# Feature products of a graph-attention layer in 32-column tiles, four side by side, in place of 64-column tiles

## The chip, the core and the metric

The kernel runs on one core of a Trainium2 chip. The metric is the device time of one execution in microseconds (us). Before the change it is 2252.53 us, the median of three runs (2251.53 to 2253.24).

## What is computed

Four graph layers follow each other on N = 2708 nodes with 256 features; each adds its result to its input and normalizes the sum over the features. The change lies in the last of them, a graph attention with 4 heads of 64 channels:

```
x = _layernorm(x + _L3_gnn_ref(x, adj, W, a_src, a_dst, bias))

def _L3_gnn_ref(x, adj, W, a_src, a_dst, bias):
    h = (x @ W).reshape(n, 4, 64)
    s_src = jnp.einsum('nhc,hc->nh', h, a_src)
    s_dst = jnp.einsum('nhc,hc->nh', h, a_dst)
    e = jax.nn.leaky_relu(s_src[:, None, :] + s_dst[None, :, :], 0.2)
    e = jnp.where((adj > 0.5)[:, :, None], e, -1e9)
    alpha = jax.nn.softmax(e, axis=0)
    return jnp.einsum('ijh,ihc->jhc', alpha, h).reshape(n, 256) + bias
```

All is float32, apart from masks. The first three layers are a gated layer with three attention heads, a normalized adjacency product and a second attention layer; they fill the first 1870 us or so and stay as they are.

## The kernel before, in words

Each engine runs a list of instructions written out by hand, and semaphores tie the lists together. In the last layer the exponentials are factored: an edge's weight is the larger of two products of a factor of the source node and one of the target node, times a mask. A factor of the source is moved out of the weight, into the projected features and into the denominators' operand.

The work is divided into three **sweeps** over the target nodes (`CW` = 3, column chunks `c` of 1024, 1024 and 660 targets) and, in each sweep, 22 **units**, one for each tile `t` of 128 source nodes (the last tile has 20). A unit is `n = c * 22 + t`, 66 in all. In each unit:

- SP loads the unit's strip of the adjacency into one of three buffers. ACT turns it into a mask (`above` L1466, `masked` L1473). In sweep 1 ACT also scales the tile's projected features (L1459), and before that it lays the source factors out as `g3`, 32 equal columns for each head.
- VectorE makes the weights of the four heads, `PM3` (L2085), each 128 sources by the sweep's targets, in one of three buffers: unit n waits until TensorE has finished unit n - 3 (`l3_mm`, L2078), and for the mask. Each head raises `l3_p`.
- TensorE multiplies. The **features**, L1150: for heads 0 and 1, then 2 and 3, and for each half of the targets (512 and 512 columns, in sweep 3 512 and 148), the stationary operand is 64 columns of `proj3`, one head, and the moving one that head's weights. The two heads of a pair write partitions 0 to 63 and 64 to 127 of one bank. The **denominators**, L1161: for each half, four products with 32 columns of `g3`, one for each head, which write partitions 0 to 31, 32 to 63 and so on of a bank. The last one raises `l3_mm`.

The trace has two weight loads and two products for each float32 product of the program, so a unit has 16 records of loads and 16 of products on L1150, and as many on L1161. Products of tiles that lie side by side in the array run at the same time.

The sums stay in six banks over a sweep: features of heads 0 and 1 in banks 0 and 1, of heads 2 and 3 in 2 and 3, denominators in 4 and 5. At a sweep's first unit each pair of banks is opened by a product of full width with zeros (`opened`, L880), after ACT has copied out the banks of the sweep before (`chunk_out`, L1481, after the last unit's `l3_mm`). After units 3, 7, 11 and 15 of sweeps 2 and 3 TensorE transposes two tiles of the sweep before back (`backs`, L1134), of which VectorE makes divisors (`divisors`, L2040 to L2046), ACT scaled rows (L1490), POOL a term for nodes without edges (L821, L823), and VectorE sums, statistics and the normalized rows (`added` L2053 on, `normed` L2068 on). VectorE does these between its weights, after units 5, 7 and 9 of each group of four. The tiles of the last sweep are finished behind the last unit.

Of the kernel before, what the change touches and what calls it, by code (L numbers as in the profile page):

```python
# [18 lines left out]
P = 128  # L19
# [5 lines left out]
T = -(-N // R)  # L25
# [12 lines left out]
C2, C3 = D // H2, D // H3  # L38
DQ = P // H3
# [10 lines left out]
BANK = 512  # L50
# [33 lines left out]
def kp(t):  # L84
    return R if t < T - 1 else TAIL
# [50 lines left out]
def wide(c):  # L136
    return min(WW, N - c * WW)
# [34 lines left out]
def build(nc, x, adj, gat_W, gat_a, e_Wih, e_Whh, e_bih, e_bhh, n_Wih, n_Whh, n_bih, n_bhh,  # L172
          W1, b1, W2, a2, W3, a_src, a_dst, b3, out):
    V, S, G, PE = nc.vector, nc.scalar, nc.gpsimd, nc.tensor
# [13 lines left out]
    with ExitStack() as ctx:  # L188
# [5 lines left out]
        def sb(*shape, dt=F32):  # L194

            n = int(np.prod(shape))
            words = n if dt == F32 else (n + 1) // 2 if dt == BF16 else (n + 3) // 4
            a = arena[:, top[0]:top[0] + words]
            top[0] += words + words % 2
            assert top[0] <= ARENA, top[0]  # L200
            if dt != F32:
                a = a.bitcast(dt)[:, 0:n]
            if len(shape) > 1:
                names = "abcd"[:len(shape)]
                a = a.rearrange(f"p ({' '.join(names)}) -> p {' '.join(names)}", **dict(zip(names, shape)))
            return a
# [143 lines left out]
        proj3 = sb(T, D + 2 * H3)  # L350
# [5 lines left out]
        PM3 = sb(3, H3, WW)  # L356
# [6 lines left out]
        def bank(i, n=1):  # L363
            return psum[:, i:i + n, :].rearrange("p b n -> p (b n)")
# [92 lines left out]
        def pair_at(n, first):  # L457

            c, t = divmod(n, T)
            if c and t >= first and (t - first) % 4 == 0 and (t - first) // 4 < DT // 2:  # L460
                return (c - 1) * DT // 2 + (t - first) // 4
            return None
# [415 lines left out]
        def opened(b):  # L878

            PE.matmul(bank(b), zrow[:, 0:P], zrow, start=True, stop=True)  # L880

        @block.tensor
        def _(pe):
# [137 lines left out]
            for n in range(UNITS):  # L1021
                c, t = divmod(n, T)
# [32 lines left out]
            for t in range(T):  # L1055
# [4 lines left out]
                for g in range(2):  # L1060
# [4 lines left out]
                    for kk in range(KD):  # L1065
# [5 lines left out]
                                        skip_group_check=True)  # L1071
# [25 lines left out]
            for n in range(UNITS):  # L1097
                c, t = divmod(n, T)
# [9 lines left out]
            for n in range(UNITS):  # L1108
                c, t = divmod(n, T)
# [5 lines left out]
                for h in range(H2):  # L1115
                    pe.wait_ge(l2_p, n * H2 + h + 1)
                    for r, nr in enumerate(blocks2(c)):
# [3 lines left out]
                                        start=k // 3 not in begun, stop=t == T - 1, skip_group_check=True)  # L1121
# [7 lines left out]
            def backs(v):  # L1129
                if v:  # L1130
                    pe.wait_ge(fin_scaled, v)
                for i, g in enumerate((2 * v, 2 * v + 1)):
                    for k in range(RAW3):
                        ins = PE.transpose(bank(6 + i)[0:kp(g), k * P:(k + 1) * P], rawT3[:, k, g % DT * R:g % DT * R + kp(g)], ident)  # L1134
                ins.then_inc(back_ps, 1)
            for n in range(UNITS3):
                c, t = divmod(n, T)
                halves = [(v, min(BANK, wide(c) - v * BANK)) for v in range(-(-wide(c) // BANK))]
                for h in range(0, H3, 2):
                    if t == 0:  # L1140
                        if c:
                            pe.wait_ge(l3_read, RAW3 * (c - 1) + h // 2 + 1)
                        for v, w in halves:
                            opened(h + v)
                    if c == 0:
                        pe.wait_ge(l3_scaled, t + 1)
                    pe.wait_ge(l3_p, n * H3 + h + 2)
                    for v, w in halves:
                        for g in range(2):
                            PE.matmul(bank(h + v)[g * C3:(g + 1) * C3, 0:w], proj3[0:kp(t), t, (h + g) * C3:(h + g + 1) * C3],  # L1150
                                      PM3[0:kp(t), n % 3, h + g, v * BANK:v * BANK + w], start=False, stop=t == T - 1, skip_group_check=True)
                if t == 0:
                    if c:
                        pe.wait_ge(l3_read, RAW3 * c)
                    else:
                        pe.wait_ge(l3_g, 1)
                    for v, w in halves:
                        opened(4 + v)
                for v, w in halves:
                    for h in range(H3):  # L1160
                        ins = PE.matmul(bank(4 + v)[h * DQ:(h + 1) * DQ, 0:w], g3[0:kp(t), t, h, :],  # L1161
                                        PM3[0:kp(t), n % 3, h, v * BANK:v * BANK + w], start=False, stop=t == T - 1, skip_group_check=True)
                ins.then_inc(l3_mm, 1)
                v = pair_at(n, 3)
                if v is not None:
                    pe.wait_ge(l3_read, RAW3 * c)
                    backs(v)
# [353 lines left out]
        def dve_project(dve, i, pieces, between={}):  # L1521

            _, _, proj_ps, proj_ok = projs[i]
            for q, t in enumerate(ORDER if i == 2 else range(T)):
                if q in between:
                    between[q]()
                dve.wait_ge(proj_ps, q + 1)
                for dst, b, lo, hi in pieces:
                    src = bank(2 * (q % 2) + b)[0:kp(t), lo:hi]
                    if len(dst.shape) == 4:  # L1530
                        src = src.rearrange("p (h f) -> p h f", h=H2)
                    ins = V.tensor_copy(dst[0:kp(t), t], src)
                ins.then_inc(proj_ok, 1)
            dve.wait_ge(proj_ok, T)
# [4 lines left out]
        def head_vector(link, wv, av, dst):  # L1539

            _, hh, ff = wv.shape
            pv = prod[:, 0:hh * ff].rearrange("p (h f) -> p h f", h=hh)
            link(V.tensor_tensor(pv, wv, av, ALU.mult))
            link(V.tensor_reduce(dst, pv, AX_X, ALU.add))

        @block.vector
        def _(dve):
# [143 lines left out]
            def arguments(n):  # L1691
                c, t = divmod(n, T)
                w = wid(c)
                if t == 0:
                    shifts_there(dve, c)
                if n >= 3:
                    dve.wait_ge(s["mm_done"], n - 2)
                dve.wait_ge(s["blk_in"][n % 4], strips_landed(n))
                for h in range(H0):
                    if t < T - 1:  # L1700
                        part, step = slice(0, R), e_step[0:R, h, t:t + 1]
                    else:
                        part = slice(h * GAP, (h + 1) * GAP)
                        step = e_tail[part, 2:3]
                    ins = V.tensor_scalar(head_of(n, h)[0], strips[n % 4][part, 0:w], 0.0, step, ALU.is_lt, ALU.mult)
                ins.then_inc(gen_arg, 1)
                dve.wait_ge(gen_arg, 2 * n + 1)
                for h in range(H0):
                    out, source, _, _ = head_of(n, h)
                    ins = V.tensor_tensor(out, source, out, ALU.subtract)  # L1710
                ins.then_inc(gen_arg, 1)
# [410 lines left out]
```

## Time and profile before

| | |
|---|---|
| median of three runs | 2252.53 us |
| lowest, highest | 2251.53, 2253.24 us |
| profiled execution: span from first to last instruction | 2246.4 us |
| its own device time | not recorded |
| TensorE products busy, share of the span | 2101.5 us, 94% |
| VectorE busy | 1555.7 us, 69% |
| ACT busy | 949.8 us, 42% |
| last layer's sweeps 1, 2, 3 (first feature product to last product) | 1873.1 to 1998.8, 2000.9 to 2129.7, 2131.8 to 2222.9 us |

Times in the trace are us from the start of the span. A product's records begin when it enters the array, and their ends are modelled: they overlap the next ones, so that the distance of starts tells the pace, not the length of a record. PE stands for TensorE's products, PEld for its weight loads, DVE for VectorE, SPq and the like for queues. "issue" is a time in which an engine waited for nothing that the profile shows.

### The profile page before, as it was taken

The numbers are of one execution on the slowest core, as the hardware profiler recorded it, in microseconds if no ns is written. First come the engines' busy times: TensorE is split into PE (matmuls) and PEld (weight loads), VectorE is DVE, ScalarE is ACT, GpSimd is POOL, SyncE is SP. The second block draws the span as 40 slices with busy tenths as digits, with TensorE's granted clock in tenths as the row PEclk, the third lists the DMA queues.
The fourth block names the chain that finished last, engine by engine and source line by source line (L and its number), as shares of the span: only waits on it lengthen the run. The fifth ranks groups of instructions, "written<-read, shape, count | busy, mean of one in ns | idle before, by whom it ended". The sixth has DMA issues, their size and how long they took to land.

```text
span 2246.4 us, 26319 instructions
## 1 busy us (share of the span) xinstructions
PE 2101.5 (94%) x9738; PEld 1157.4 (52%) x9747; DVE 1555.7 (69%) x2623; ACT 949.8 (42%) x1459; POOL 118.3 (5%) x169
## 2 busy tenths in 40 slices
PE   7999999799999988889999999999899987999996
PEld 4556665344444454445555534556899962222232
DVE  4665547696967577743678863444899957879987
ACT  2222215687878687855222210001021246544342
POOL 0000000000000000000001010000010030002011
PEclk9999999899999999999999999999899988999997
DMA  7665634455454545553000034451110115323231
GB/s 235 217 206 181 217 102 195 155 178 183 170 191 142 183 156 199 171 181 127 1 0 1 0 90 129 131 130 27 51 33 20 38 40 194 87 85 90 71 86 39
DMA packets 133167, 265.56 MB, mean 118 GB/s; under 512 B 15258, under 2 KB 62904, under 8 KB 130200
## 3 DMA queue, kind: packets, MB, share of 16 engines
q1 hardware_dynamic: 114712, 234.50, 33.1%
q10 hardware_dynamic: 18324, 29.34, 3.5%
q8 instruction: 78, 1.28, 0.2%
q14 instruction: 53, 0.43, 0.1%
HBM read 220.43 MB, written 43.36 MB: 117 GB/s over the span
## 4 chain that ended last, share of the span: by engine, by line
PE 61%; DVE 22%; ACT 11%; issue 4%; DMA 2%; SPq 1%; POOL 0%; DVEq 0%; ACTq 0%; POOLq 0%
PE banks L1034 13%; PE banks L937 9%; PE banks L1085 9%; PE banks L1150 8%; PE banks L1119 6%; PE banks L1161 4%; ACT arena L1266 4%; DVE arena L1658 3%; PE banks L926 3%; DVE arena L2013 3%; ACT arena L1302 2%; DVE arena L2085 2%; PE banks L978 2%; PE banks L849 2%; ACT arena L1295 1%
## 5 line engine op out<-in xcount | busy, mean ns | idle before, releaser
L1034 PE MATMUL banks<-arena 128*128 128x512 f32 (+2 forms) x1512 | 598.1, 553 | 45.1 <-DVE arena L1741 45.1
L1034 PEld LDWEIGHTS banks<-arena 128*128 128x128 f32 x1512 | 286.0, 193 | 346.4 <-issue 266.3
L1741 DVE TENSOR_TENSOR arena<-arena 128x1536 f32<-128x1536 f32 (+4 forms) x132 | 201.5, 1527 | 173.6 <-ACT arena L1302 147.0
L2085 DVE SCALAR_TENSOR_TENSOR arena<-arena 128x1024 f32<-128x1024 f32 (+3 forms) x264 | 293.6, 1180 | 33.1 <-PE banks L1161 25.9
L1150 PE MATMUL banks<-arena 128*64 128x512 f32 (+3 forms) x1056 | 222.5, 561 | 13.0 <-DVE arena L2085 12.9
L1119 PE MATMUL banks<-arena 128*124 128x129 f32 (+2 forms) x1936 | 219.1, 275 | 10.6 <-DVE arena L2013 10.5
L937 PE MATMUL banks<-arena 128*128 128x512 f32 (+4 forms) x528 | 225.7, 549 | 0.2 <-ACT arena L1207 0.2
L1119 PEld LDWEIGHTS banks<-arena 128*124 128x124 f32 (+2 forms) x1936 | 216.1, 187 | 13.6 <-issue 7.5
L1085 PE MATMUL banks<-arena 128*128 128x512 f32 (+4 forms) x528 | 207.4, 547 | 5.0 <-DVE arena L1842 3.7
L1658 DVE CUSTOM_DVE_ANT_0 arena<-arena 128x2708 f32<-128x2708 bf16 (+1 forms) x66 | 196.3, 2974 | 3.3 <-DVE arena L1652 3.3
L1295 ACT ACTIVATE arena<-arena 128x512 f32<-128x512 f32 (+4 forms) x264 | 162.2, 660 | 80.1 <-PE banks L1034 77.5
L1266 ACT ACTIVATE arena<-arena 128x2708 f32<-128x2708 f32 (+1 forms) x66 | 168.5, 2554 | 46.5 <-DVE arena L1669 46.5
L1302 ACT ACTIVATE arena<-arena 128x1536 f32<-128x1536 f32 (+4 forms) x132 | 170.7, 1293 | 40.7 <-DVE arena L1723 39.9
L2013 DVE SCALAR_TENSOR_TENSOR arena<-arena 128x496 f32<-128x496 f32 (+2 forms) x264 | 173.1, 713 | 16.3 <-PE banks L1119 15.0
L1207 ACT COPY arena<-banks 128x512 f32<-128x512 f32 (+4 forms) x132 | 70.6, 535 | 224.3 <-PE banks L926 223.8
L1085 PEld LDWEIGHTS banks<-arena 128*128 128x128 f32 (+1 forms) x528 | 99.0, 190 | 104.6 <-issue 72.5
L1150 PEld LDWEIGHTS banks<-arena 128*64 128x64 f32 (+1 forms) x1056 | 69.8, 138 | 158.1 <-issue 137.0
L1607 DVE TENSOR_SCALAR arena<-arena 128x512 bf16<-128x512 f32 (+4 forms) x132 | 52.2, 395 | 127.2 <-ACT arena L1207 126.9
L1828 DVE TENSOR_SCALAR arena<-arena 128x512 uint8<-128x512 f32 (+4 forms) x132 | 51.9, 399 | 95.5 <-DMA arena<-adj_T 95.3
L1161 PE MATMUL banks<-arena 128*32 128x512 f32 (+3 forms) x1056 | 117.3, 562 | 0.0
L937 PEld LDWEIGHTS banks<-arena 128*128 128x128 f32 (+1 forms) x528 | 90.0, 190 | 52.3 <-issue 36.4
L1473 ACT ACTIVATE arena<-arena 128x1024 bf16<-128x1024 f32 (+1 forms) x66 | 69.1, 1047 | 73.7 <-DVE arena L2085 73.7
(223 smaller groups left out, 2214.3 us busy)
## 6 DMA issues: line engine op xcount, KB each, us to landing
arena<-hw_rows SPq DMA_DIRECT2D x126, 384.0 KB, 3.2
arena<-adj_T SPq DMA_DIRECT2D x126, 256.0 KB, 3.3
arena<-in_adj SPq DMA_DIRECT2D x17, 1354.0 KB
arena<-in_adj SPq DMA_DIRECT2D x42, 512.0 KB
adj_T<-arena ACTq DMA_DIRECT2D x63, 256.0 KB, 2.2
arena<-adj_T SPq DMA_DIRECT2D x84, 192.0 KB, 3.1
arena<-in_adj SPq DMA_DIRECT2D x15, 1024.0 KB
arena<-in_adj SPq DMA_DIRECT2D x15, 768.0 KB
```

The costliest lines, as they stand in the source:

```text
L937: PE.matmul(bank(2 * (c % 2) + f)[:, 0:w], xnat[0:k, t, f * P:(f + 1) * P], AT[0:k, n % 4, 0:w], start=t == 0, stop=t == T - 1)
L1034: ins = PE.matmul(bank(2 * (c % 2) + f)[:, 0:wid(c)], hs[0:R, m % 3, h * D + f * P:h * D + (f + 1) * P], E[0:R, n % 3, h, 0:wid(c)], start ...
L1085: ins = PE.matmul(bank(2 * (c % 2) + f)[:, 0:wid(c)], xd[0:kp(t), t, f * P:(f + 1) * P], strips1[0:kp(t), n % 4, 0:wid(c)], start=t == 0, ...
L1119: ins = PE.matmul(bank(b0 + k // 3)[0:nr, (k % 3) * (C2 + 1):(k % 3 + 1) * (C2 + 1)], PM2[0:kp(t), n % 3, h, r * R2:r * R2 + nr], proj2[0: ...
L1150: PE.matmul(bank(h + v)[g * C3:(g + 1) * C3, 0:w], proj3[0:kp(t), t, (h + g) * C3:(h + g + 1) * C3], PM3[0:kp(t), n % 3, h + g, v * BANK:v ...
L1161: ins = PE.matmul(bank(4 + v)[h * DQ:(h + 1) * DQ, 0:w], g3[0:kp(t), t, h, :], PM3[0:kp(t), n % 3, h, v * BANK:v * BANK + w], start=False, ...
L1266: S.activation(srow[0:kp(i), j % 2, :], srow[0:kp(i), j % 2, :], ACT.Exp, bias=negm[0:kp(i), h, i:i + 1], accum_out=den[0:kp(i), h, i:i + ...
L1302: S.activation(e, e, ACT.Exp, scale=-1.0).then_inc(s["y_ok"], 1)
L1658: link(V.tensor_tensor_reduce(out=srow[0:nr, sl, :], in0=bias[0:nr, :], in1=e_bc[0:nr, h, :], scale=1.0, scalar=3 * NEG, op0=ALU.add, op1= ...
L1741: V.tensor_tensor(e, e, a, ALU.mult).then_inc(s["p_ok"], 1)
L2013: V.scalar_tensor_tensor(PM2[0:k, n % 3, h, 0:w], r2_bc[0:k, h, c * CW2:c * CW2 + w], smalls[0:k, 4, h * T + t:h * T + t + 1], mask2[0:k, ...
L2085: V.scalar_tensor_tensor(PM3[0:k, n % 3, h, 0:w], r3_bc[0:k, h, c * WW:c * WW + w], smalls[0:k, 4, h * T + t:h * T + t + 1], mask3[0:k, n ...
```

## The change

The feature products of a head pair are cut into four tiles of 32 columns (`P // DQ` = 4, `DQ` = 32) instead of two of 64. Tile q takes columns q * 32 to q * 32 + 31 of the pair's 128 columns of `proj3`, the weights of head h for q = 0, 1 and of head h + 1 for q = 2, 3, and writes partitions q * 32 on of the same bank. Banks, order of the loops, waits and semaphores stay; each feature product of the program becomes two with half its columns, so L1150 issues 16 products a unit instead of 8. The line of the denominators becomes L1162.

```diff
                     pe.wait_ge(l3_p, n * H3 + h + 2)
                     for v, w in halves:
-                        for g in range(2):
-                            PE.matmul(bank(h + v)[g * C3:(g + 1) * C3, 0:w], proj3[0:kp(t), t, (h + g) * C3:(h + g + 1) * C3],
-                                      PM3[0:kp(t), n % 3, h + g, v * BANK:v * BANK + w], start=False, stop=t == T - 1, skip_group_check=True)
+                        for q in range(P // DQ):
+                            PE.matmul(bank(h + v)[q * DQ:(q + 1) * DQ, 0:w], proj3[0:kp(t), t, h * C3 + q * DQ:h * C3 + (q + 1) * DQ],
+                                      PM3[0:kp(t), n % 3, h + q * DQ // C3, v * BANK:v * BANK + w], start=False, stop=t == T - 1,
+                                      skip_group_check=True)
```

## Rows read from the trace of the kernel before

**Rows 1.** The page's heading.

```profile
span 2246.4 us, 26319 instructions
```

**Rows 2.** Groups by line and shape, 1870 to 2246.4 us: count, busy us, mean ns, idle before.

```profile
L1150 PE MATMUL banks<-arena 128*64 128x512 f32 x840 | 203.6, 613 | 13.0 <-DVE arena L2085 12.9
L1161 PE MATMUL banks<-arena 128*32 128x512 f32 x840 | 103.3, 600 | 0.0
```

**Rows 3.** Busy time of each engine (records), granted clock, DMA share; sweeps 1 and 2.

```profile
core 0: us, PE busy (x) PEld busy (x) DVE busy (x) ACT busy (x) POOL busy (x), PEclk, DMA share, GB/s
1904.00:1991.00 87.00, 87.00 (x516) 23.63 (x512) 78.00 (x65) 45.84 (x80) 0.00 (x0) 1.00 0.33 97
2027.00:2121.00 94.00, 94.00 (x558) 26.82 (x558) 93.07 (x116) 42.34 (x70) 15.21 (x16) 1.00 0.30 84
```

**Rows 4.** Who waited for whom, 1870 to 1991.5 us: us in total, times, longest.

```profile
DVE arena L2085 <- PE banks L1161: 9.0, 16, 0.6
```

**Rows 5.** Weight loads in order of time, sweep 1, one unit: start us, us, engine, line.

```profile
1936.92 0.20 PEld L1150 LDWEIGHTS banks<-arena 128*64 128x64 f32 x4 [0.84 <-issue]
1937.40 0.14 PEld L1150 LDWEIGHTS banks<-arena 128*64 128x64 f32 x2 [0.29 <-issue]
...
1939.55 0.14 PEld L1150 LDWEIGHTS banks<-arena 128*64 128x64 f32 x2 [0.29 <-issue]
1940.51 0.16 PEld L1161 LDWEIGHTS banks<-arena 128*32 128x32 f32 x8 [0.81 <-issue]
1940.96 0.13 PEld L1161 LDWEIGHTS banks<-arena 128*32 128x32 f32 x4 [0.30 <-issue]
1941.40 0.13 PEld L1161 LDWEIGHTS banks<-arena 128*32 128x32 f32 x4 [0.30 <-issue]
1942.37 0.20 PEld L1150 LDWEIGHTS banks<-arena 128*64 128x64 f32 x4 [0.84 <-issue]
```

**Rows 6.** VectorE in order of time, 2009 to 2027 us, sweep 2's first units.

```profile
2020.57 4.87 DVE L2085 SCALAR_TENSOR_TENSOR arena<-arena 128x1024 f32<-128x1024 f32 x4 [0.57 <-PE banks L1161]
2026.79 0.23 DVE L2040 COPY arena<-banks 128x4 f32<-128x4 f32 x2 [1.35 <-PE banks L1134]
```

**Rows 7.** VectorE in order of time, 2108 to 2118 us, from unit 42 on.

```profile
2111.57 7.25 DVE L2085 SCALAR_TENSOR_TENSOR arena<-arena 128x1024 f32<-128x1024 f32 x6
```

**Rows 8.** TensorE in order of time, 2110 to 2118 us: unit 42's first products.

```profile
2116.28 1.94 PE L1150 MATMUL banks<-arena 128*64 128x512 f32 x8
```

**Rows 9.** The chain that ended last, in order of time, sweep 3: start us, us, what.

```profile
2144.12 1.25 PE banks L1161 x16
2145.37 2.38 PE banks L1150 x16
...
2161.12 5.80 DVE arena L2085 x7
...
2178.79 5.80 DVE arena L2085 x7
```

**Rows 10.** VectorE in order of time, 2127 to 2152 us: border of sweeps 2 and 3.

```profile
2129.80 3.36 DVE L2085 SCALAR_TENSOR_TENSOR arena<-arena 128x660 f32<-128x660 f32 x4 [1.21 <-PE banks L1161]
2138.18 3.36 DVE L2085 SCALAR_TENSOR_TENSOR arena<-arena 128x660 f32<-128x660 f32 x4 [5.03 <-PE banks L1161]
2141.81 3.36 DVE L2085 SCALAR_TENSOR_TENSOR arena<-arena 128x660 f32<-128x660 f32 x4 [0.28 <-PE banks L1161]
...
2149.84 0.23 DVE L2040 COPY arena<-banks 128x4 f32<-128x4 f32 x2 [1.05 <-PE banks L1134]
```

**Rows 11.** The chain again: sweep 3's first features, a pair of transposes, the end.

```profile
2131.90 2.40 PE banks L1150 x8
...
2149.00 0.82 PE banks L1134 x6
...
2216.71 1.33 PE banks L1150 x8
```

**Rows 12.** Busy time and granted clock at the border of sweeps 1 and 2.

```profile
1994.80:2005.00 10.20, 8.66 (x29) 1.61 (x28) 6.48 (x6) 6.15 (x7) 0.00 (x0) 0.50 0.06 8
```

**Rows 13.** The products of the layer before (L1119) alone: PE and PEld busy (records).

```profile
1622.00:1642.00 20.00, 20.00 (x182) 19.88 (x181) 1.00 0.15 39
```

## The prediction, made before the changed kernel ran

> **What bounds the kernel now.** The profiled execution spans 2246.4 us [rows 1]; the median of the three timed runs is 2252.53 us, 6.1 us above it. The execution's own time was not recorded, so I treat 6.1 us as what lies around the span and make the sum against 2252.5. All that the change touches is the last layer, from 1870 us to the end; I read that stretch by line and shape first. Two groups hold what the change is about [rows 2]: the feature products (L1150) and the denominators (L1161). The page calls TensorE busy throughout, but its busy share doesn't tell which engine sets the end of each sweep. The three sweeps have different answers, so I read the stages with the busy times of each engine [rows 3] and the waits of VectorE in order of time.
>
> In sweep 1 (1873 to 1999 us) VectorE is busy for 78 of 87 us and TensorE for all of them [rows 3]. VectorE waits for TensorE's last denominator product (its buffers are three deep) 0.57 to 0.58 us in each of the last 16 or so units, 9.0 us in all [rows 4]. TensorE is the bound, at 5.45 us a unit (1936.92 to 1942.37 in [rows 5]) against VectorE's 4.87 [rows 6].
>
> In sweep 2 VectorE gets extra work from tile 5 on (divisors, additions, norms). From 2027 to 2121 us it is busy 93.07 of 94 us [rows 3]: it is bound by itself, and lives on its lead over TensorE. The lead is shrinking. VectorE began the weights of unit 42 at 2111.57 us (six heads in 7.25 us [rows 7], so the first two were there by about 2114.0), and TensorE took them up at 2116.28 [rows 8]: some 2.2 us of lead are left.
>
> In sweep 3 (wide columns 512 and 148) TensorE needs 1.25 + 2.38 = 3.63 us a unit, and VectorE comes back to the same place of its cycle of four units after 2178.79 - 2161.12 = 17.67 us [rows 9], 4.42 a unit. So VectorE is the bound, once its waits at the border of the sweeps are over (1.21, 5.03, 0.28, once more 0.27, and 1.05 us [rows 10]).
>
> **What the width costs.** The records of the weight loads show the pace of the array, as a step's last loads start together with its products [rows 5]. The 64-column tiles run two side by side: steps of 0.43 us (from 1937.40 to 1939.55 five steps in 2.15). The 32-column tiles run four side by side: a step of 0.44 (1940.96 to 1941.40). So two 64s and four 32s fill the same 128 columns at nearly the same pace; there is **no gain in the streaming** itself, and eight feature steps a unit stay eight. What differs lies at the changes of width:
> - 64 to 32: the last 64-step begins at 1939.55 and would end at 1939.98; the first 32-product begins at 1940.51, 0.10 us late. The step after it takes 0.45 instead of 0.43, 0.02 more.
> - 32 to 64: the last 32-step begins near 1941.83; the next unit's first 64-product begins at 1942.37, 0.11 us late, and its first step takes 0.48 (1936.92 to 1937.40), 0.05 more.
>
> Together 0.28 us of the 5.45; twelve steps of 0.43 are 5.16, and the rest is this. Within the features the bank, the head pair and VectorE's semaphore change without such a gap, and the gap at 64 to 32 is there although no semaphore is raised in between: so it belongs to the width. After the change all twelve steps of a unit have width 32, and both changes vanish.
>
> **The price of the new steps.** There are twice as many feature products and weight loads: 32 more records a unit, in the same eight steps. The bounds for such a step are the 64-step (0.430) and the 32-step (0.44 as printed); the denominators' four steps with the two late starts make 1.86 us (1940.51 to 1942.37), which puts a plain one at 0.432 to 0.435. I take 0.433, so eight steps cost 0.025 us a unit more, and a unit saves 0.28 - 0.025 = 0.255 us. The Trainium skill (TensorE: Matmul & The Clock Gate, section "Measured speedup vs the span model") gives about 4 ns to each further tile side by side, which speaks against the change: eight steps with two further tiles are an estimated 0.064 us a unit, the saving 0.216, and the sum below would end about 1 us lower. The printed steps are too coarse to exclude this.
>
> **The sum, along what is late.**
> 1. Up to the first transposes back (L1134, after unit 25) TensorE is the bound. Units 1 to 21 and 23 to 25 are entered from 32 columns and change inside; unit 22 is opened between by full-width products (L880) and saves almost nothing, as unit 0. 24 x 0.28 - 26 x 0.025 = 6.1 us. VectorE's copy of the divisors, which waits 1.35 us for that transpose [rows 6] and before it 0.58 us a unit, moves up by the same 6.1.
> 2. From there VectorE runs 94 us without a wait, and that does not shrink. TensorE could gain 18 x 0.255 = 4.6 us more by the end of sweep 2, but only until it has eaten VectorE's lead, 2.2 us. Where it starves, VectorE's next weights release it. So the end of sweep 2 on TensorE comes 6.1 + 2.1 = 8.2 us earlier, not 10.7.
> 3. Here the lead pays: at the border VectorE waits 7.8 us for TensorE [rows 10]. It has room for all of it, and units 45 to 47 save another 3 x 0.28 less 4 x 0.025, 0.7. The divisors' copy at 2149.84 moves up by 8.9.
> 4. The rest of sweep 3 is VectorE's and keeps its length. At the very end TensorE is last again: after 2216.71 one and a half units follow (6.25 us, the features at 1.33 of [rows 11] and then 1.25, 2.37 and 1.3 as in [rows 9]), with one entry and two changes inside: 0.28 + 0.12 - 0.04 = 0.36.
>
> Sum: 8.9 + 0.36 = 9.3 us; 2252.5 - 9.3 = 2243.2. Nothing is costed on ACT, SP or POOL: ACT is busy 46 of 87 us in sweep 1, DMA a third [rows 3], and no engine waits for them there in steady flow.
>
> The granted clock is the loose end. At the borders of the sweeps it is at the lower level, 1.2 GHz (0.50), for 10.2 us [rows 12], from the middle of the unit of tile 21, which has 20 rows instead of 128. The rows of that unit stay 20, so I expect the same; a stretch longer or shorter by a third would move the end by 10.2 / 3 / 2 = 1.7 us at each of two borders. Add the step price (0.430 to 0.44 makes 9.9 down to 7.5 us) and that the lead may be eaten with less or more grace (1 us). That gives 2239.5 to 2247.5 for the forecast itself.
>
> **Rivals.**
> - *Issue becomes the bound, slower.* TensorE would have to take 96 records a unit: in 5.18 us that is 54 ns each, in sweep 3 in 3.36 us 35 ns. The densest long flow in the trace is the layer before: 182 products and 181 loads in 20 us, 55 ns a record [rows 13]. If this is a limit of issue and not the length of those products, a unit of sweep 3 lasts 96 x 55 = 5.28 us, above VectorE's 4.42; it decides from 46 ns a record. Sweep 3 would be TensorE's: it begins at 2131.90 [rows 11], 8.2 earlier, and lasts 22 x 5.28 + 4 x 0.82 for the transposes back, to 2243.2, where it now ends at 2216.71 + 6.25 = 2223.0: 20 us slower, 2273. Against it: the 32 denominator records of a sweep-3 unit take 1.25 us [rows 9], 39 ns each, though a queue filled before could do that. 6 in 100. The Trainium skill (TensorE: Matmul & The Clock Gate, "Wait — 56ns, not 53.3ns?") names about 62 ns of sequencer time for each MATMUL in one mode of decoding; for 48 a unit that would be an estimated 2.98 us and would not bind, and no run here shows it alone.
> - *The two new tiles of a head disturb each other.* The denominators' four tiles read four different heads; the new ones read two heads, each twice at the same time. From a step of 0.454 (5.45 / 12) nothing is left, at 0.46 the kernel is slower by 66 x 8 x 0.006, 3 us at most: 2253 to 2256. No row shows such a pair. 5 in 100, half of it within 0.2%.
> - *The gap is not the width's.* If the 0.10 and 0.11 us belong to the change of the program's loop, only the loads' 0.07 goes, less 0.025: 0.045 x 26 and little more, 2251. 5 in 100. Against it stands that the head pairs within L1150 pass without a gap.
> - *Only sweep 1 arrives.* VectorE's lead turns out to be worth nothing at the border, and 6.1 us remain: 2246.4. 6 in 100; the 5.03 us of waiting speak against it.
>
> **How the numbers follow.** The forecast has 78 in 100, and nearly all of it below 2248.0. A measurement of this kernel tells from no change what is over about 0.2%, 4.5 us. Faster: 78 + 6, less 1 for the forecast's own upper tail, 0.83. Same: the gap (5), half of the pairs (2.5), the tail (1), 0.09. Slower: 6 + 2.5, 0.08. The range goes from 2239.5 to 2249, which leaves out the rivals at 2251 and above (about 15 in 100) and little else.
>
> **What would show it.** In the profile after: feature products in the form 128x32, 2112 of them; sweep 1's units at 5.18 to 5.20 us in the chain, with no gap between the two lines; VectorE's wait per unit in sweep 1 down from 0.58 to about 0.3; late in sweep 2 TensorE waiting for VectorE, which it does nowhere in that stretch now [rows 3]; VectorE's 5.03 us wait at the border down to 3 or less; sweep 3 unchanged in length. A unit of 5.4 or more, or a unit of over 4.4 in sweep 3, would make the prediction wrong.

## The result, and the profile after

The changed kernel takes 2239.74 us, the median of four runs (2238.29 to 2242.18), against 2252.03 us for the kernel before. The ratio is 0.9944, with a 95% interval of 0.9930 to 0.9958: 12.6 us faster, between 9.5 and 15.8. The prediction had 9.3 us less and a range of 2239.5 to 2249.0. The median lies 0.2 us inside its lower end, and the ratio applied to 2252.03 gives 2239.4, 0.1 us outside. So the direction and most of the sum held, and a part of the gain of some 3 us is missing in the forecast. It is found below. Every ratio here is of fast executions; one execution of a variant (5549.3 us, with half the tiles narrow) was a slow one and is left out of its ratio.

The profiled execution of the changed kernel took 2238.43 us with a span of 2236.7 us: 1.7 us lie around the span, and this is so in every profile that follows. The 6.1 us that the prediction took for that were wrong; with 1.7 us the execution of before whose span is 2246.4 us [rows 1] comes to about 2248, below its median. This matters for reading spans: VectorE's first weight of the last layer comes between 1870.3 and 1875.8 us in the ten traces, although the code ahead of it is the same (in two variants two memsets more). So I read times inside the last layer from VectorE's first weight (1870.47 us before, 1873.16 us after).

```profile
span 2236.7 us, 28431 instructions
```

First the pace, in the weight loads of one unit of sweep 1 (start us, us, engine, line), to be laid beside [rows 5]:

```profile
1937.38 0.17 PEld L1150 LDWEIGHTS banks<-arena 128*32 128x32 f32 x4 [0.26 <-issue]
1937.82 0.17 PEld L1150 LDWEIGHTS banks<-arena 128*32 128x32 f32 x4 [0.26 <-issue]
...
1939.10 0.17 PEld L1150 LDWEIGHTS banks<-arena 128*32 128x32 f32 x4 [0.26 <-issue]
1939.54 0.17 PEld L1162 LDWEIGHTS banks<-arena 128*32 128x32 f32 x4 [0.26 <-issue]
...
1940.82 0.17 PEld L1162 LDWEIGHTS banks<-arena 128*32 128x32 f32 x4 [0.26 <-issue]
1941.25 0.17 PEld L1150 LDWEIGHTS banks<-arena 128*32 128x32 f32 x4 [0.26 <-issue]
```

From 1937.38 to 1941.25 there are nine steps of 0.43 us, straight through both turns, features to denominators and back. The starts that were 0.10 and 0.11 us late are gone, and twelve such steps make 5.16 us where 5.45 were.

Then the busy times of each engine in sweep 1 and in the part of sweep 2 where VectorE is the bound, beside [rows 3] (same columns), and VectorE's waits in sweep 1 beside [rows 4]:

```profile
1904.00:1991.00 87.00, 87.00 (x814) 34.55 (x808) 83.36 (x70) 49.85 (x88) 0.00 (x0) 1.00 0.36 105
2027.00:2110.00 83.00, 81.53 (x750) 24.99 (x742) 82.17 (x105) 35.94 (x57) 10.18 (x13) 1.00 0.32 90
```

```profile
DVE arena L2086 <- PE banks L1162: 3.4, 12, 0.3
```

In sweep 1 TensorE is still the bound, and VectorE's wait a unit went from 0.58 to 0.29 us. In sweep 2 TensorE is no longer busy throughout: it has caught up with VectorE and waits for it, as its timeline at the end of the sweep shows (unit 42 begins at 2108.47, and both of its head pairs wait for VectorE's weights; [rows 8] before):

```profile
2108.47 1.93 PE L1150 MATMUL banks<-arena 128*32 128x512 f32 x16 [0.25 <-DVE arena L2086]
2110.86 1.93 PE L1150 MATMUL banks<-arena 128*32 128x512 f32 x16 [0.46 <-DVE arena L2086]
```

VectorE over the border to sweep 3, beside [rows 10]:

```profile
2116.34 9.89 DVE L2086 SCALAR_TENSOR_TENSOR arena<-arena 128x660 f32<-128x660 f32 x12
2129.27 10.04 DVE L2086 SCALAR_TENSOR_TENSOR arena<-arena 128x660 f32<-128x660 f32 x12 [3.04 <-PE banks L1162]
2140.05 0.23 DVE L2041 COPY arena<-banks 128x4 f32<-128x4 f32 x2 [0.75 <-PE banks L1134]
```

Of the 7.8 us that it waited there, 3.8 are left (3.04 + 0.75). Behind that sweep 3 is VectorE's, with the same cycle as in [rows 9], and TensorE's units there, which are only for a moment on the chain, last 1.11 + 2.23 = 3.34 us:

```profile
2131.43 1.11 PE banks L1162 x16
2132.54 2.23 PE banks L1150 x32
...
2151.35 5.80 DVE arena L2086 x7
...
2169.03 5.80 DVE arena L2086 x7
```

2169.03 - 2151.35 = 17.68 us, where 17.67 were. Next, the granted clock at the two borders, beside [rows 12]:

```profile
1993.90:2000.70 6.80, 5.53 (x23) 1.06 (x28) 4.67 (x4) 6.79 (x7) 0.00 (x0) 0.50 0.15 34
2120.20:2127.00 6.80, 5.66 (x31) 1.32 (x36) 6.03 (x8) 5.45 (x7) 0.00 (x0) 0.50 0.22 54
```

The lower level, 1.2 GHz, lasts 6.8 us at each border instead of 10.2. This is what the sum had not foreseen.

At the very end the clock falls before TensorE is done, which it doesn't in the kernel before. The granted clock in the last unit's denominators, after and before, and these denominators on the chain of the changed kernel:

```profile
2212.40:2213.20 0.80, 0.80 (x12) 0.21 (x4) 0.00 (x0) 0.00 (x0) 0.00 (x0) 0.50 0.44 145
2222.20:2222.90 0.70, 0.70 (x16) 0.12 (x4) 0.00 (x0) 0.00 (x0) 0.00 (x0) 1.00 0.42 142
```

```profile
2211.76 1.50 PE banks L1162 x16
```

They take 1.50 us; with 32 columns in sweep 3 alone, where the clock is still at 2.4 GHz there, they take 1.16.

Where the time of the last layer went, as the distance from VectorE's first weight:

| | before | after | gain | forecast |
|---|---|---|---|---|
| first copy of divisors in sweep 2 | 156.32 | 147.96 | 8.4 | 6.1 |
| first copy of divisors in sweep 3 | 279.37 | 266.89 | 12.5 | 8.9 |
| last instruction | 375.9 | 363.5 | 12.4 | 9.3 |

### The profile page after: what moved, and what is told of

The parts are those of the page before. It is cut to its first block, busy times and chain, and to the rows that moved or that the text cites. A ratio compares the mean times of both kernels' runs of the same rounds, so it can differ in the third digit from the quotient of the medians.

```text
span 2236.7 us, 28431 instructions
## 1 busy us (share of the span) xinstructions
PE 2087.2 (93%) x10794; PEld 1169.3 (52%) x10803; DVE 1554.2 (69%) x2623; ACT 950.4 (42%) x1459; POOL 117.4 (5%) x169
## 4 chain that ended last, share of the span: by engine, by line
PE 57%; DVE 25%; ACT 12%; issue 4%; DMA 2%; SPq 1%; POOL 0%; DVEq 0%; ACTq 0%; POOLq 0%
PE banks L1034 13%; PE banks L1085 9%; PE banks L937 9%; PE banks L1119 6%; PE banks L1150 5%; DVE arena L2086 5%; ACT arena L1267 4%; DVE arena L1659 3%; PE banks L926 3%; DVE arena L2014 3%; PE banks L1162 3%; ACT arena L1303 2%; PE banks L978 2%; PE banks L849 2%; ACT arena L1296 1%
## 5 line engine op out<-in xcount | busy, mean ns | idle before, releaser
L1150 PE MATMUL banks<-arena 128*32 128x512 f32 (+3 forms) x2112 | 222.7, 557 | 16.8 <-DVE arena L2086 16.8
L1119 PE MATMUL banks<-arena 128*124 128x129 f32 (+2 forms) x1936 | 219.2, 275 | 10.4 <-DVE arena L2014 10.2
L1119 PEld LDWEIGHTS banks<-arena 128*124 128x124 f32 (+2 forms) x1936 | 216.2, 187 | 13.4 <-issue 7.2
L2014 DVE SCALAR_TENSOR_TENSOR arena<-arena 128x496 f32<-128x496 f32 (+2 forms) x264 | 172.3, 709 | 16.8 <-PE banks L1119 15.8
L1150 PEld LDWEIGHTS banks<-arena 128*32 128x32 f32 (+1 forms) x2112 | 71.7, 111 | 153.7 <-issue 133.0
L1162 PE MATMUL banks<-arena 128*32 128x512 f32 (+3 forms) x1056 | 114.1, 546 | 0.0
```

What stands on the lines that cost most here:

```text
L1119: ins = PE.matmul(bank(b0 + k // 3)[0:nr, (k % 3) * (C2 + 1):(k % 3 + 1) * (C2 + 1)], PM2[0:kp(t), n % 3, h, r * R2:r * R2 + nr], proj2[0: ...
L1150: PE.matmul(bank(h + v)[q * DQ:(q + 1) * DQ, 0:w], proj3[0:kp(t), t, h * C3 + q * DQ:h * C3 + (q + 1) * DQ], PM3[0:kp(t), n % 3, h + q * D ...
L2014: V.scalar_tensor_tensor(PM2[0:k, n % 3, h, 0:w], r2_bc[0:k, h, c * CW2:c * CW2 + w], smalls[0:k, 4, h * T + t:h * T + t + 1], mask2[0:k, ...
```

## The experiments

Eight kernels, each timed in rounds beside the kernel before. For the first four, a table behind them reads the layer at the same three points of each trace. In the variants the lines of the weights and of the denominators shift by one to three.

### One sweep at a time

The width of the feature tiles is chosen by the sweep, `c` being 0, 1 or 2 for sweeps 1, 2 and 3. The edit for sweep 1 alone, against the kernel before:

```diff
-                        for g in range(2):
-                            PE.matmul(bank(h + v)[g * C3:(g + 1) * C3, 0:w], proj3[0:kp(t), t, (h + g) * C3:(h + g + 1) * C3],
-                                      PM3[0:kp(t), n % 3, h + g, v * BANK:v * BANK + w], start=False, stop=t == T - 1, skip_group_check=True)
+                        cw = DQ if c == 0 else C3
+                        for q in range(P // cw):
+                            PE.matmul(bank(h + v)[q * cw:(q + 1) * cw, 0:w], proj3[0:kp(t), t, h * C3 + q * cw:h * C3 + (q + 1) * cw],
+                                      PM3[0:kp(t), n % 3, h + q * cw // C3, v * BANK:v * BANK + w], start=False, stop=t == T - 1,
+                                      skip_group_check=True)
```

> 32-column feature tiles in sweep 1 alone; sweeps 2 and 3 keep 64 columns. My theory (each pair of width changes costs TensorE 0.28 to 0.29 us a unit, and only what is late on TensorE counts): sweep 1's units last 5.16 us instead of 5.45, twenty-one of them; VectorE waits for TensorE up to the border, so all of it arrives: 5.8 to 6.3 us faster, about 2246. A rival in which the gain comes with TensorE's work wherever it is done (0.29 us times 22 units in every sweep) gives 6.4 here as well, so this run alone doesn't tell them apart; it is the base of the comparison.

Measured: ratio 0.9970 (0.9959 to 0.9982), 6.8 us faster.

> 32-column feature tiles in sweep 2 alone. My theory: three units before the first transposes back arrive whole (0.9 us); after that VectorE bounds the sweep and TensorE only eats its lead of some 2.2 us, which comes back at the border to sweep 3: about 3 us faster in all, 2249. The rival in which all of TensorE's saving arrives: 22 x 0.29 = 6.4 us faster, 2246. VectorE's lead at unit 42 should be down from 2.2 us to about 0.

Measured: ratio 0.9985 (0.9976 to 0.9993), 3.4 us faster. TensorE eats the lead and then waits for VectorE in sweep 2; these are who-waited-for-whom rows, 2027 to 2119 us:

```profile
PE banks L1151 <- DVE arena L2087: 1.9, 4, 0.7
```

> 32-column feature tiles in sweep 3 alone. My theory: units 45 to 47 and the last one and a half units are TensorE's, the rest is VectorE's: 0.8 + 0.4 = 1.2 us faster, 2251, within the noise. The rival in which all of TensorE's saving arrives: 6.4 us faster, 2246. If issue of 96 records a unit were a limit of 46 ns or more, this kernel would be slower than before.

Measured: ratio 0.9997 (0.9987 to 1.0007), 0.7 us, no difference that the runs can tell. In its trace the layer is 1.3 us shorter, so all but 1.3 us of TensorE's saving in sweep 3 is hidden behind VectorE.

The three gains add up to 10.9 us; the whole change gains 12.6 us in the first series and 14.0 (below) in the second. The rival of an equal gain in each sweep falls by sweeps 2 and 3: 6.4 us was asked of each, and 3.4 and 0.7 came.

### The changed kernel again

> The changed kernel unchanged, a second profile and more runs. If the shorter stretches at the lower clock at the two borders (6.8 us in the first profile of it, 10.2 in that of before) belong to the change, they are 6.8 again; if they are a matter of where they fall, one or both are 10.2 and the layer is 1.7 us longer for each. Time 2238 to 2242 either way; 12 us faster by my sum with the step of 0.43 and both short stretches, 9.3 to 10 without them.

Measured: ratio 0.9938 (0.9925 to 0.9951), median 2237.39 us. In its trace the low clock lasts 6.8 us at both borders, as in the first one. The points of the layer in the five traces:

| | first copy in sweep 2 | first copy in sweep 3 | end | low clock at border 1, 2 |
|---|---|---|---|---|
| before | 156.3 | 279.4 | 375.9 | 10.2, 10.2 |
| sweep 1 alone | 147.5 | 268.8 | 365.4 | 6.8, 6.8 |
| sweep 2 alone | 155.6 | 275.3 | 371.9 | 10.2, 6.8 |
| sweep 3 alone | 156.2 | 278.3 | 374.6 | 10.2, 10.2 |
| changed, again | 147.8 | 266.7 | 363.4 | 6.8, 6.8 |

(us from VectorE's first weight.) The short stretches aren't bound to the width of the tiles at the border: with 32 columns in sweep 1 alone, border 2, where the tiles on both sides are 64 wide, has 6.8 as well. They seem to go with the time at which the border comes. Sweep 1 alone gains 10.5 us in its trace, where 6.0 were expected: 3.4 of the rest are the two short stretches, and 1.4 the layer's start, where the low clock ended at 5.4 us behind the first weight instead of 8.2. But the execution that was traced was the fastest of six (2237.40 us, the median 2244.0), and the timed gain, 6.8 us (4.1 to 9.2), lies below the 9.4 that 6.0 and two short stretches make. So no run shows that its stretches are short in every execution; of the changed kernel both traces show it. Sweep 2 alone: 4.0, of which 1.7 are one short stretch; that leaves 2.3, against 3 expected. Sweep 3 alone: 1.3, and 1.2 expected; 1.0 of it is there at the first copy in sweep 3, and 0.3 comes at the very end, where TensorE's last one and a half units take 5.95 us instead of 6.25.

### The same number of changes of width, with half the tiles narrow

The width is chosen by the head pair (`h` is 0 or 2). The edit is against the variant with sweep 1 alone:

```diff
-                        cw = DQ if c == 0 else C3
+                        cw = DQ if h == 2 else C3
```

> Heads 2 and 3 in four 32-column tiles, heads 0 and 1 in two 64-column tiles, in all sweeps. There are still two changes of width a unit, of the same kind (32 to 64 before heads 0 and 1, 64 to 32 before heads 2 and 3 instead of before the denominators). My theory: a unit lasts 5.45 us as before, time 2251, no change. A rival in which narrow tiles themselves run faster, or in which the cost sits at the turn from features to denominators: half of the change's gain or more, 5.3 us a unit, 6 us faster.

Measured: ratio 0.9998 (0.9989 to 1.0006). Its weight loads in sweep 1 show the same two late starts, the second of them now inside the features:

```profile
1941.89 0.20 PEld L1151 LDWEIGHTS banks<-arena 128*64 128x64 f32 x4 [0.84 <-issue]
1942.38 0.14 PEld L1151 LDWEIGHTS banks<-arena 128*64 128x64 f32 x2 [0.29 <-issue]
1942.81 0.14 PEld L1151 LDWEIGHTS banks<-arena 128*64 128x64 f32 x2 [0.29 <-issue]
1943.77 0.16 PEld L1151 LDWEIGHTS banks<-arena 128*32 128x32 f32 x8 [0.81 <-ACT arena L1461]
1944.22 0.13 PEld L1151 LDWEIGHTS banks<-arena 128*32 128x32 f32 x4 [0.30 <-issue]
1944.65 0.13 PEld L1151 LDWEIGHTS banks<-arena 128*32 128x32 f32 x4 [0.30 <-issue]
1945.09 0.13 PEld L1163 LDWEIGHTS banks<-arena 128*32 128x32 f32 x4 [0.30 <-issue]
...
1947.35 0.20 PEld L1151 LDWEIGHTS banks<-arena 128*64 128x64 f32 x4 [0.84 <-issue]
```

The step before 1943.77 began near 1943.24 and 0.10 us are lost there, between two lots of features, while 1944.65 to 1945.09, from features to denominators, is a plain step. 1941.89 to 1947.35 is a unit of 5.46 us. The gap follows the change of width and not the turn of the loop or the bank, and narrow tiles by themselves gain nothing. The low clock lasts 10.2 us at both borders here.

### Twice the changes of width

The width is chosen by the half of the targets (`v`), again against the variant with sweep 1 alone:

```diff
-                        cw = DQ if c == 0 else C3
+                        cw = DQ if v == 1 else C3
```

> 64-column tiles for the first 512 targets of each head pair, 32-column tiles for the second half, in all sweeps: four changes of width a unit (32 to 64, 64 to 32, 32 to 64, 64 to 32) instead of two. My theory: twice the cost of the changes, 5.16 + 4 x 0.145 = 5.74 us a unit. Sweep 1 ends 21 x 0.29 = 6.1 us later than before, sweep 2 another 5 to 6 (TensorE at 5.94 us a unit with the transposes back is now slower than VectorE at 5.79), sweep 3 stays VectorE's (3.92 us a unit against 4.42) with 1.5 more at its ends: 12 to 14 us slower than before, 2264. The rival in which the changes of width cost nothing: 2245 to 2251.

Measured: ratio 1.0055 (1.0042 to 1.0068), 12.4 us slower than before; 2265.05 us. Weight loads in sweep 1:

```profile
1936.81 0.16 PEld L1151 LDWEIGHTS banks<-arena 128*32 128x32 f32 x8 [0.81 <-issue]
1937.81 0.20 PEld L1151 LDWEIGHTS banks<-arena 128*64 128x64 f32 x4 [0.84 <-ACT arena L1461]
1938.81 0.16 PEld L1151 LDWEIGHTS banks<-arena 128*32 128x32 f32 x8 [0.81 <-issue]
...
1941.53 0.20 PEld L1151 LDWEIGHTS banks<-arena 128*64 128x64 f32 x4 [0.84 <-issue]
1942.54 0.16 PEld L1151 LDWEIGHTS banks<-arena 128*32 128x32 f32 x8 [0.81 <-issue]
```

Two steps of one width and the change behind them take 1.00 us instead of 0.86, and a unit lasts 1942.54 - 1936.81 = 5.73 us: 5.16 + 4 x 0.1425. The cost doubles with the number of changes, so a change of width costs 0.14 us on the mean of both kinds. The low clock lasts 10.2 us at border 1 and 6.8 at border 2, so a short stretch also comes in a kernel that is slower than before.

### The 20 rows of the last tile, and the clock

What remained were the stretches at the lower clock. They begin in or right behind the unit of tile 21, whose operands have 20 rows. This variant of the changed kernel multiplies that tile over all 128 rows, of which 108 are zeros in the stationary operands:

```diff
+            link(V.memset(proj3[:, T - 1, :], 0.0))
+            link(V.memset(g3[:, T - 1].rearrange("p h q -> p (h q)"), 0.0))
             dve_project(dve, 2, ((proj3, 0, 0, D + 2 * H3),), {
...
-                            PE.matmul(bank(h + v)[q * DQ:(q + 1) * DQ, 0:w], proj3[0:kp(t), t, h * C3 + q * DQ:h * C3 + (q + 1) * DQ],
-                                      PM3[0:kp(t), n % 3, h + q * DQ // C3, v * BANK:v * BANK + w], start=False, stop=t == T - 1,
+                            PE.matmul(bank(h + v)[q * DQ:(q + 1) * DQ, 0:w], proj3[0:R, t, h * C3 + q * DQ:h * C3 + (q + 1) * DQ],
+                                      PM3[0:R, n % 3, h + q * DQ // C3, v * BANK:v * BANK + w], start=False, stop=t == T - 1,
...
-                        ins = PE.matmul(bank(4 + v)[h * DQ:(h + 1) * DQ, 0:w], g3[0:kp(t), t, h, :],
-                                        PM3[0:kp(t), n % 3, h, v * BANK:v * BANK + w], start=False, stop=t == T - 1, skip_group_check=True)
+                        ins = PE.matmul(bank(4 + v)[h * DQ:(h + 1) * DQ, 0:w], g3[0:R, t, h, :],
+                                        PM3[0:R, n % 3, h, v * BANK:v * BANK + w], start=False, stop=t == T - 1, skip_group_check=True)
```

> The changed kernel, with the last source tile multiplied over all 128 rows: the 108 rows behind the 20 real ones are zeros in the projected features and in the denominators' operand (two memsets on VectorE ahead of the projection), so the sums are the same and only TensorE's records of that tile have 128 rows. If the clock falls at the borders because of the unit with 20 rows, it stays at 2.4 GHz there: of 6.8 us at the lower level 1.5 are TensorE's pause, so each border gives back (6.8 - 1.5) / 2 = 2.6 us, two borders 5.3: 2233, 5 us faster than the changed kernel. If it falls because of TensorE's pause of 1.5 us for ACT's copy of the banks, nothing changes: 2238.

Measured: 2232.97 us, ratio to the kernel before 0.9916 (0.9902 to 0.9931). Busy time of each engine and granted clock (the 1.00) at border 1, in this kernel:

```profile
1993.00:2003.00 10.00, 8.89 (x74) 2.15 (x70) 6.16 (x6) 7.45 (x8) 0.00 (x0) 1.00 0.25 63
```

and TensorE's timeline there:

```profile
1992.21 1.95 PE L1162 MATMUL banks<-arena 128*32 128x512 f32 x16
1995.26 0.61 PE L880 MATMUL banks<-arena 128*128 128x512 bf16 x2 [1.10 <-ACT arena L1482]
1995.80 1.93 PE L1150 MATMUL banks<-arena 128*32 128x512 f32 x16
1997.65 0.60 PE L880 MATMUL banks<-arena 128*128 128x512 bf16 x2
```

The pause for ACT's copy is still there, 1.10 us, and the clock is at 2.4 GHz throughout; at border 2 no low stretch is left either. So the unit with 20 rows made the clock fall, and not the pause: the variants with half the tiles narrow and with twice the changes have pauses of 1.11 us too, and the clock fell there. The distance from first weight to end is 357.5 us, 6.0 less than the changed kernel's (5.3 expected). At the price of two memsets this kernel is faster than both others, by 0.84% or 19 us against the kernel before.

> The kernel before (64-column tiles), with the last source tile over all 128 rows in the same way. If the 20 rows make the clock fall: of 10.2 us at the lower level at each border 1.5 are pause, (10.2 - 1.5) / 2 = 4.3 us given back at each, 8.7 in all: 2242.5. The difference of this kernel to the changed one with full rows is then the gain of the width alone, without the clock's part: 9.0 us by my sum. If the pause makes it fall: 2251.

Measured: 2243.25 us, ratio 0.9960 (0.9947 to 0.9973); the layer takes 367.6 us in its trace, 8.3 less than before (8.7 expected). The clock at border 1, over the same times from the start of the span as in [rows 12]; tile 21's unit lies in it, from 1996.61 to 2002.13:

```profile
1994.80:2005.00 10.20, 9.07 (x58) 2.45 (x58) 9.05 (x9) 2.80 (x4) 0.00 (x0) 1.00 0.01 2
```

At border 2 it stays at 2.4 GHz as well. With the clock's fall out of both kernels the width alone is worth 2243.25 - 2232.97 = 10.3 us, 367.6 - 357.5 = 10.1 us in the traces.

## Why the prediction came out as it did

The step that failed is the time at the lower clock at the borders, which the sum took to stay at 10.2 us each; 6.8 us were measured at both, worth some 3 us together. A smaller part is the price of the new steps. The mechanism, what the width costs and where it counts, held. Point by point, by the prediction's own steps:

- **What the width costs** (0.10 + 0.02 and 0.11 + 0.05 us a unit): right. Both gaps are gone from the trace; half the tiles narrow with two changes left gains nothing, and four changes cost twice as much, 5.73 us a unit. The Trainium skill (TensorEngine Tiling (Array Packing), section "Key Properties") says that a change of tiling mode, not of tile alone, drains TensorE; the traces fit that, with 0.10 to 0.11 us before the first product of the new width and 0.02 to 0.05 us more in its first step. That the array drains in this time no run shows by itself.
- **The price of the new steps**: too high by a little. Where 0.433 us stood for a step of four tiles, the changed kernel shows 0.430, no longer than a step of two. So the 0.025 us a unit that I took off were not due: 26 x 0.025 = 0.65 us by the end of sweep 2's first four units, 0.8 in the whole sum. The some 4 ns for each further tile of the Trainium skill's rule (TensorE: Matmul & The Clock Gate, section "Measured speedup vs the span model") don't appear in the distance between steps here.
- **Sum, point 1**: 6.1 us forecast, 8.4 in the trace: 0.65 from the step, and 1.7 from the clock.
- **Point 2**: right. TensorE eats the lead of 2.2 us and waits; sweep 2 alone gains 2.3 us besides the clock's part, of about 3 expected.
- **Point 3**: right in its mechanism. VectorE's waits at the border took the lead up, and 1.7 us of clock more. 12.5 - 8.4 = 4.1 us were gained between the two copies; 8.9 - 6.1 = 2.8 forecast.
- **Point 4**: sweep 3 kept its pace, 17.68 us for four units. The 0.36 us at the very end did not show, 12.4 against 12.5 before it, because the clock fell 0.9 us before the last product was done: the last unit's denominators take 1.50 us where sweep 3 alone has 1.16, and 1.53 in the second trace. Sweep 3 alone gains the 0.3 us. Why the clock falls earlier there isn't known. Both traces of the changed kernel have one more stretch at 1.2 GHz, of 3.4 us (2198.7 to 2202.1 in the first). It costs nothing: the last unit begins 69.4 us after the first copy of divisors in sweep 3, and 69.3 in sweep 3 alone, which has no such stretch.
- **The granted clock** is the term that was mis-sized. The prediction expected the same 10.2 us at each border and priced a third less at 1.7 us, but only as a width of the range; it came at both borders, in both traces of the changed kernel: 3.4 us by that price. With it and the step of 0.430 us the sum is 9.3 + 0.8 + 3.4 = 13.5, where the trace of the layer shows 12.4 and the timed ratios 12.6 and 14.0. The price was a little high. At the two copies of divisors the full rows give back 4.4 and 4.3 us of the kernel before, one for each border, and 2.8 and 3.0 of the changed one, which is 2.9 us less and not 3.4; most of what is left of the difference lies at the very end (point 4). The range was too narrow for its own terms: 2252.5 - 9.9 - 3.4 - 1 = 2238.2, and its end stood at 2239.5.
- **Without the clock** the sum holds at each of its points. These are gains of 32 columns over 64 in the layer, with full rows in both kernels, beside the forecast with the step of 0.430 us (nothing taken off for it):

| | forecast, step of 0.430 us | full rows, measured |
|---|---|---|
| first copy of divisors in sweep 2 | 24 x 0.28 = 6.7 | 6.8 |
| first copy of divisors in sweep 3 | + 2.1 + 3 x 0.28 = 9.7 | 9.6 |
| last instruction | + 0.40 = 10.1 | 10.1 |

- **Why 6.8 and not 10.2** is shown only in part. That the clock falls because of the unit with 20 rows is shown. That a border which comes at another time has a shorter stretch is what the traces of sweep 1 alone, sweep 2 alone and twice the changes suggest, since it isn't bound to the width beside the border. In the kernel before the fall came at 1994.8 us, 3.4 us after the first product of that unit (1991.4), and its denominators ran at half pace; in the changed one it came at 1993.9, behind the unit (1988.3 to 1993.6). The same shows over all 16 borders of the eight traces with 20 rows: the eight short stretches begin 4.2 to 5.8 us after the first product of that unit, seven of the eight long ones 2.6 to 3.6 us after it and one 4.2. What decides the moment wasn't tried by itself, and neither was any number of rows between 20 and 128.

The rivals:

- *Issue becomes the bound*: fallen. TensorE takes 96 records in 3.34 us in sweep 3, 35 ns each, for three units one after the other. So the 55 ns a record of [rows 13] were no limit of issue; that they were the length of those products is what remains, and wasn't tried.
- *The two new tiles of a head disturb each other*: fallen; a step is 0.43 us.
- *The gap is not the width's*: fallen, by half the tiles narrow.
- *Only sweep 1 arrives*: fallen; sweep 2 alone gains 3.4 us (1.6 to 5.4 by its interval), and 2.3 in its trace without the clock's part.

## What to carry to other kernels

Where small matmuls of several tile widths alternate, the change of width has a price of its own, here 0.14 us each on the mean; cutting the wider ones down to the narrower width cost nothing here, where four tiles of 32 columns fill the same 128 columns as two of 64. Such a gain counts only where TensorE is late: of some 19 us of TensorE time saved (66 x 0.29) some 10 arrived, as VectorE bound the rest. And a ragged last tile is worth a look at the granted clock behind it: filling it up to 128 rows with zeros took 6.0 us (32 columns) and 8.3 us (64 columns) off the layer here.

## What the runs showed of the hardware that I had not expected

- In or right behind a unit of 12 steps (5.2 us) that TensorE takes without a pause, but with 20 rows instead of 128, the granted clock fell from 2.4 to 1.2 GHz for 6.8 or 10.2 us, at both borders of all eight traces that had it; with 128 rows, 108 of them zeros in the stationary operand, it didn't fall in either kernel, although a pause of 1.1 us follows.
- Four tiles of 32 columns, of which two and two read the same moving columns at the same time, run in the same 0.430 us a step as two tiles of 64.
- TensorE took 96 records of loads and products in 3.34 us, 35 ns each, over three units.
